# The low half of x by TensorE and ScalarE, the value bias and the token order by TensorE, and no copy of the largest scores, in the projection and the linear q, k, v stages

## The chip, the cores and the metric

One NeuronCore of a Trainium2 chip runs the whole program. The time is the device time of one launch in microseconds, and it is compared as a median of several launches. The engines are TensorE (PE; its weight loads are listed as PEld), VectorE (DVE), ScalarE (ACT), GpSimd (POOL) and SyncE (SP), which here only issues DMAs. TensorE's clock has two levels, 1.2 and 2.4 GHz; "granted clock" is its share of full speed (0.5 or 1).

## The reference

Four sublayers, each `x = x + layernorm(f(layernorm(x)))`, on x of 8 x 1024 x 256 floats (8192 tokens):

```python
x = x + ln(softmax_attention(ln(x)) @ w_proj)        # 16 heads of 16, causal
x = x + ln(moe64(ln(x)))                             # sigmoid scores, 6 of 64 experts, shared expert
x = x + ln(linear_attention(ln(x)) @ W_out + b_out)  # q, k = elu(...) + 1.0001, causal sums
x = x + ln(moe8(ln(x)))                              # softmax scores, 4 of 8 experts, shared expert
```

Two pieces matter here. After the first attention comes its projection, the residual sum, the next layernorm and the choice of six experts:

```python
scores = sigmoid(ln(x) @ router_weight.T)
_, top_idx = top_k(scores + expert_bias, 6)
probs = take(scores, top_idx) / (sum + 1e-20)
```

And the linear attention begins with its q, k and v:

```python
qkv = ln(x) @ W_qkv + b_qkv
q = elu(q * 16 ** -0.5) + 1.0001
k = elu(k) + 1.0001
```

## The kernel before

The program is seven phases, one after the other, with a barrier between them. Two of them are touched: `phase_project_route` (tiles named `prj_`) and `phase_linear_qkv` (tiles named `lqk_`). Both walk over 16 blocks of 512 tokens (8 batches x 2 halves). Each engine has its own instruction list, written by hand as a function `stages(...)`, and `pipeline` runs it so that several blocks are in flight: in one step of `prj` the stages a, b, c, d work on four successive blocks, in one step of `lqk` the stages a, b, c on three. Semaphores alone tie the lists together, and each engine does its list strictly in the written order; the order of the work is therefore exactly the order of the code, for SP's DMA issues too.

Products are made to near full precision from two halves. `xh` is x rounded to fp32r, `xl` is what is left (x - xh), and `product` adds three fp32r matmuls per 128 rows of contraction (high x high, high x low, low x high). The normal x comes out of a layernorm with tokens on the partitions (`xn`), TensorE turns it (8 transposes of 128 x 128, `xn_ready` to `xn_turned`) into `t_ps` in PSUM, ScalarE copies `t_ps` to `xh`, and VectorE then forms `xl = t_ps - xh` (lines 1052 and 1743), signalled by `xl_ready`.

**A step of prj, engine by engine.** TensorE: the projection of block b into `y_ps` (24 matmuls of 256 columns, waits for `al_ready`), the router logits of block d into `l_ps` (24 matmuls of 64 columns, waits for `xl_ready`), the 8 transposes of block c, then `r_ps` for the mask of block d (waits for `choice_ready`). ScalarE: the sigmoid `sc` (waits for the logits), four normalisations `xn`, the high half `ah` of the attention output, four normalisations `yn`, `xh`, and the copy `rt` of `r_ps`. VectorE: statistics of x and of y, two scalings `nmr`, the division `att`, the choice of the experts (`choose`: bias added into `sb`, MAX8, a copy of the K largest values into `pick`, MATCH_REPLACE8, mask), `al = att - ah`, `xl`, and the weights (`weigh`). `pick` holds the six largest scores and two values of 3e38; `sb` has two spare columns that hold 3e38, which the replacing operation uses up in their place.

**A step of lqk.** TensorE: q and k of block c (`qk`: 4 x 6 matmuls of 512 columns, waits for `xl_ready`), the 8 transposes of block b, v of block c (`vp`: 24 matmuls of 256 columns), then 8 transposes of phi(k) of block c (line 1832), which write `t_ps` too and so wait for `xl_ready` of block b, and for `phi_done`. ScalarE: exponentials 0 and 1 of `qk`, four normalisations `xn`, exponentials 2 and 3, four normalisations `yn`, `xh`, and the copy `kt` of the turned phi(k). VectorE: the residual sum `x2` (waits for `yn`), the statistics of x2 and of the summed expert output `a`, two scalings, twice (min of the exponentials, two `phi`), the bias added to v (`vo`, line 1735), and `xl` (line 1743). POOL sums the three parts of `a`. A block's tokens lie as four runs of 128 (`t`, `q`: token 4 q + t stands at column 128 t + q); `phi` has to be stored in token order, and VectorE restores it when it reads `qk` and `ex`:

```python
def in_order(a):
    return a.rearrange("p (t q) -> p q t", t=TPB)
...
e.scalar_tensor_tensor(phi[:, j, k].rearrange("p (q t) -> p q t", t=TPB),
                       in_order(qk[:, k]), bqk1[:, k:k + 1], in_order(ex[:, k]),
                       ALU.add, ALU.max).then_inc(phi_done, 1)
```

SP, in one step of lqk: the store of x2 and the four loads of the next block (after `inputs_used`), the store of v (after `vo_ready`), and the stores of phi(q), phi(k) and kt (after `kt_ready`). Since the list is strict, the loads of a step stand behind the kt stores of the step before.

## Time and profile before

| | us |
|---|---|
| median of three launches | 3262.55 (3261.11 to 3276.6) |
| the profiled launch: its own time | 3258.48 |
| the profiled launch: its span, first to last instruction | 3256.8 |
| PE busy in the span | 2842.0 (87%) |
| DVE busy | 2225.7 (68%) |
| ACT busy | 1603.0 (49%) |
| POOL busy | 731.5 (22%) |

prj takes its 16 blocks between about 1130 and 1344 us of the span, lqk between about 1693 and 1956 us. A period is the time between two successive steps of such a stage: the first `xl` of prj starts at 1135.2 and the sixteenth at 1336.8, and in lqk they start at 1696.6 and 1939.4, so that 15 periods are 201.6 us (13.4 each) and 242.8 us (16.19 each). In the timeline rows further down the columns are: start in us, length in us (from the first start to the last end, where rows are merged with xN), engine, line, operation, output<-inputs with sizes, and in brackets the idle time of that engine just before it and what ended it. A matmul's length contains its latency, so matmuls in a stream overlap: how fast they go is read from the distance of their starts.

### The profile page before, as it was taken

Reading aid. Unit: us, or ns where it says so; the run is one execution under the profiler, and the core shown is the slowest. Engines: PE = TensorE matmul, PEld = TensorE weight load, DVE = VectorE, ACT = ScalarE, POOL = GpSimd, SP = SyncE. Lnnn points to the kernel's source line nnn. Section 1 sums busy time; section 2 is a strip of 40 time slices with the busy share of each in tenths; the row PEclk is TensorE's granted clock in tenths of the full one; section 3 lists DMA queues with packets and bytes.
Section 4 is the critical chain, followed back from the end, with each engine's and each line's share of the span. In section 5 each row is a group of like instructions: output and inputs, shape, how many; then the busy total and the mean of one; then the engine's idle time right before and its main releaser. Section 6 shows DMA issues by size and latency. Waiting matters only on the chain. (4 is left out here: it accounts for less than half of the span.)

```text
span 3256.8 us, 59136 instructions
## 1 busy us (share of the span) xinstructions
PE 2842.0 (87%) x20033; PEld 2062.9 (63%) x20033; DVE 2225.7 (68%) x6134; ACT 1603.0 (49%) x2446; POOL 731.5 (22%) x882
## 2 busy tenths in 40 slices
PE   7959999999999387689947777998399999999998
PEld 6834444444444276578836664555388888888887
DVE  6768999999997388663338883444466666666664
ACT  3506777777777244333325544544244444444443
POOL 1022222222222133247744422222000000000000
PEclk9959999999999666699968888999699999999999
DMA  6984556666662377648857867653432424243331
GB/s 244 330 153 83 108 115 112 112 112 116 112 110 65 127 270 269 214 138 225 221 165 269 296 228 228 183 162 100 132 99 74 122 65 117 78 102 92 90 86 46
DMA packets 342662, 485.87 MB, mean 149 GB/s; under 512 B 58832, under 2 KB 203248, under 8 KB 342384
## 3 DMA queue, kind: packets, MB, share of 16 engines
q1 hardware_dynamic: 331776, 468.94, 52.1%
q0 software_dynamic: 10240, 14.16, 2.3%
q8 instruction: 85, 1.39, 0.2%
q10 hardware_dynamic: 496, 0.84, 0.1%
q14 instruction: 65, 0.53, 0.1%
HBM read 278.77 MB, written 204.53 MB: 148 GB/s over the span
## 5 line engine op out<-in xcount | busy, mean ns | idle before, releaser
L551 ACT ACTIVATE att_pr<-att_e_ps 128x1024 f32<-128x1024 f32 (+2 forms) x640 | 567.3, 938 | 203.8 <-PE att_e_ps L603 203.8
L579 PE MATMUL att_m_ps<-att_ks,att_qs 63*128 63x512 f32 (+3 forms) x1536 | 465.9, 433 | 40.2 <-PEq L41 31.7
L513 DVE CUSTOM_DVE_ANT_0 att_kept<-att_m_ps,att_causal 128x256 f32<-128x256 f32 (+3 forms) x1024 | 448.5, 488 | 50.3 <-DVEq L41 21.9
L579 PEld LDWEIGHTS att_m_ps<-att_ks,att_qs 63*128 63x128 f32 x1536 | 234.3, 189 | 370.6 <-DVE att_mx L516 148.5
L492 POOL TENSOR_SCALAR_AFFINE_SELECT att_pr<-att_pr 128x256 f32<-128x256 f32 (+1 forms) x384 | 181.4, 485 | 698.0 <-PEq L594 694.5
L516 DVE TENSOR_REDUCE att_mx<-att_m_ps 128x1 f32<-128x512 f32 x512 | 323.3, 684 | 21.5 <-PE att_m_ps L579 17.5
L623 PE MATMUL att_o_ps<-att_pr,att_vs 128*32 128x512 f32 (+3 forms) x3072 | 328.7, 501 | 3.7 <-issue 2.0
L2604 ACT ACTIVATE fin_hh<-fin_hid 128x512 fp32r<-128x512 f32 x192 | 121.4, 632 | 399.8 <-DVE fin_hid L2450 302.2
L603 PE MATMUL att_e_ps<-att_qs,att_ks 64*128 64x512 f32 (+3 forms) x1536 | 269.1, 376 | 6.7 <-ACT att_pr L551 3.3
L2343 POOL TENSOR_TENSOR fin_rs<-fin_ve,fin_mhalf 128x4 f32<-128x4 f32 x48 | 48.4, 1007 | 928.6 <-POOLq L41 928.6
L2446 DVE TENSOR_TENSOR fin_hid<-fin_gate,fin_u_ps 128x512 f32<-128x512 f32 x192 | 131.5, 685 | 136.4 <-ACT fin_gate L2598 82.9
L738 PE MATMUL fin_f_ps<-fin_fhd,fin_hh 128*128 128x256 f32 x768 | 219.5, 286 | 0.2 <-DVE fin_hl L2465 0.2
L738 PE MATMUL fin_f_ps<-fin_fhd,fin_hl 128*128 128x256 f32 x768 | 216.3, 282 | 0.0
L738 PE MATMUL fin_f_ps<-fin_fld,fin_hh 128*128 128x256 f32 x768 | 216.2, 282 | 0.0
L2465 DVE TENSOR_TENSOR fin_hl<-fin_hid,fin_hh 128x512 fp32r<-128x512 f32 x192 | 132.5, 690 | 104.5 <-ACT fin_hh L2604 100.8
L1949 DVE TENSOR_TENSOR lin_am<-lin_a_ps,lin_tri 128x512 f32<-128x512 f32 x128 | 88.5, 692 | 143.5 <-PE lin_a_ps L2032 143.5
L603 PEld LDWEIGHTS att_e_ps<-att_qs,att_ks 64*128 64x128 f32 x1536 | 150.1, 187 | 38.8 <-ACT att_pr L551 13.5
L738 PE MATMUL fin_u_ps<-fin_xh,fin_fhu 128*128 128x512 f32 x384 | 153.0, 398 | 0.0
L738 PE MATMUL fin_g_ps<-fin_xh,fin_fhg 128*128 128x512 f32 x384 | 152.5, 397 | 0.0
L738 PE MATMUL fin_g_ps<-fin_xh,fin_flg 128*128 128x512 f32 x384 | 151.9, 396 | 0.0
L738 PE MATMUL fin_u_ps<-fin_xh,fin_flu 128*128 128x512 f32 x384 | 151.6, 395 | 0.0
L738 PE MATMUL fin_u_ps<-fin_xl,fin_fhu 128*128 128x512 f32 x384 | 151.5, 394 | 0.0
(332 smaller groups left out, 6921.2 us busy)
## 6 DMA issues: line engine op xcount, KB each, us to landing
fin_raw<-weights SPq DMA_DIRECT2D x32, 1024.0 KB, 9.6
att_qs<-q_high SPq DMA_DIRECT2D x128, 128.0 KB, 5.2
att_ks<-k_high SPq DMA_DIRECT2D x128, 128.0 KB, 6.5
attended<-att_ot SPq DMA_DIRECT2D x64, 256.0 KB, 8.5
acc<-att_zero SPq DMA_DIRECT2D x64, 256.0 KB, 2.2
moe_w<-w SPq DMA_DIRECT2D x128, 128.0 KB, 3.4
lqk_a<-acc SPq DMA_DIRECT2D x32, 512.0 KB, 6.0
attended<-lin_ot SPq DMA_DIRECT2D x32, 512.0 KB, 3.7
```

Source lines behind the costliest of these rows:

```text
L492: e.affine_select(out=blk, in_=blk, compare_op=ALU.is_ge, fill=0.0, base=0, pattern=lead + [[1, P]], channel_multiplier=-1).then_inc(maske ...
L513: e.tensor_tensor_reduce(kept[:, n % MBUF, 0:w], m_ps[:, n % MBUF, 0:w], causal[:, BLK - w:], 1.0, -3e38, ALU.add, ALU.max, mx[:, h, at, q ...
L516: e.reduce_max(mx[:, h, at, q:q + 1], m_ps[:, n % MBUF, 0:w], AX.X).then_inc(m_free, 1)
L551: e.activation(out, src, ACT.Exp).then_inc(exp_done, 1)
L579: e.matmul(m_ps[:, (2 * i + n) % MBUF, 0:w], qs[rows, j, p, q * P:(q + 1) * P], ks[rows, j, p, h * BLK:h * BLK + w], start=True, stop=True ...
L603: i = e.matmul(e_ps[:, s % 2, n, m * w:(m + 1) * w], ks[rows, j, p, k * P:(k + 1) * P], qs[rows, j, p, (h + 1) * BLK - w:(h + 1) * BLK], s ...
L623: i = e.matmul(o_ps[32 * hd:32 * hd + 32, BLK - w:BLK], vs[:, j, k, hd * VW:hd * VW + 32], pr[:, u % NPR, hd // 2, hd % 2, 0:w], start=k = ...
L738: i = e.matmul(out, a, b, start=first and n == 0, stop=last and n == len(terms) - 1, **kw)
L1949: e.tensor_tensor(am[:, n % 2, 0:F // 2].rearrange("p (r h) q -> p r h q", h=2), a_ps[:, 0:2, 0:2 * P].rearrange("p r (h q) -> p r h q", h=2),
L2446: product_ = e.tensor_tensor(hid[:, c % 2], gate[:, c % 2], u_ps[:, c % 2], ALU.mult)
L2465: e.tensor_tensor(hl[:, c % 3], hid[:, c % 2], hh[:, c % 3].bitcast(fp32), ALU.subtract).then_inc(hl_ready, 1)
L2604: e.activation(hh[:, c % 3], hid[:, c % 2], ACT.Copy).then_inc(hh_ready, 1)
```

## The change

In both stages:

- The turning of `xn` is no longer a transpose instruction but a plain fp32 matmul with the identity as the moving operand, which opens an accumulation group in `t_ps`. When ScalarE has read `xh` out of `t_ps`, TensorE adds `-1 * xh` to `t_ps` (two matmuls of 512 columns, stationary operand `minus`, waiting for `xh_ready`, signal `rest_ready`), and ScalarE copies what is left into `xl`. VectorE's subtraction is gone.
- These two matmuls stand at the end of TensorE's step in prj, and between v and the transposes of phi(k) in lqk. The new ScalarE copy stands last in prj's step; in lqk it stands after `xh` and `vo` and before `kt`.

In prj alone: `pick` and its copy are gone. MAX8 looks at `sb` with its two spare columns of 3e38, so that `top` holds these two and the six largest scores.

In lqk alone: the matmuls of q and k read their moving operand through `in_order`, so that `qk` and `ex` come out in token order and VectorE reads and writes plain rows. The bias of v is added by TensorE (two more matmuls of one contraction row and 256 columns for each of the four `vp` tiles), and `vo` becomes a ScalarE copy from PSUM; the new semaphore `v_read`, which SP raises, keeps TensorE from writing `vp` too early. The bias is loaded as one row, no longer as 128.

```diff
+                e.wait_ge(pe_consts, 1)
+                step(e.tensor_scalar(minus[:], ident[:], -1.0, None, ALU.mult))
                 step(e.memset(sb[:, :, E:E + 8 - K], 3e38))
...
-                        e.max(top[:, t], sb[:, t, 0:E])
+                        e.max(top[:, t], sb[:, t])
                     step.settle()
-                    step(e.tensor_copy(pick[:, :, 0:K], top[:, :, 0:K]))
 
                     for t in range(TPB):
-                        e.match_replace(rep[:, t], pick[:, t], sb[:, t], -3e38)
+                        e.match_replace(rep[:, t], top[:, t], sb[:, t], -3e38)
...
-                    if c is not None:
-                        e.wait_ge(xh_ready, 1)
-                        e.tensor_tensor(xl[:, c[1]], t_ps[:], xh[:, c[1]].bitcast(fp32), ALU.subtract
-                                        ).then_inc(xl_ready, 1)
-                        take(e, (xh_ready, 1))
...
+                    if c is not None:
+                        e.wait_ge(rest_ready, 1)
+                        e.activation(xl[:, c[1]], t_ps[:], ACT.Copy).then_inc(xl_ready, 1)
+                        take(e, (rest_ready, 1))
...
-                            i = e.transpose(t_ps[:, k, t * P:(t + 1) * P], src[:, t, k * P:(k + 1) * P], ident[:])
+                            i = e.matmul(t_ps[:, k, t * P:(t + 1) * P], src[:, t, k * P:(k + 1) * P], ident[:], start=t == 0,
+                                         stop=t == TPB - 1)
...
+                    if c is not None:
+                        e.wait_ge(xh_ready, 1)
+                        for k in range(KC):
+                            i = e.matmul(t_ps[:, k], minus[:], xh[:, c[1], k], start=False, stop=True,
+                                         skip_group_check=True)
+                        i.then_inc(rest_ready, 1)
+                        take(e, (xh_ready, 1))
...
-                                e.scalar_tensor_tensor(phi[:, j, k].rearrange("p (q t) -> p q t", t=TPB),
-                                                       in_order(qk[:, k]), bqk1[:, k:k + 1], in_order(ex[:, k]),
-                                                       ALU.add, ALU.max).then_inc(phi_done, 1)
-                        e.wait_ge(v_ready, 1)
-                        for f in range(2):
-                            cols = slice(f * P, (f + 1) * P)
-                            i = e.tensor_tensor(vo[:, j, f].rearrange("p t (h d) -> p t h d", d=VW)[:, :, :, 0:HD],
-                                                vp[:, :, cols].rearrange("p t (h d) -> p t h d", d=HD),
-                                                bv[:, cols].rearrange("p (h d) -> p h d", d=HD).unsqueeze(1)
-                                                .broadcast_to((P, TPB, NH // 2, HD)), ALU.add)
-                        i.then_inc(vo_ready, 1)
-                        take(e, (exp_ready, 4), (v_ready, 1))
-                    if b is not None:
-                        e.wait_ge(xh_ready, 1)
-                        e.tensor_tensor(xl[:, b[1]], t_ps[:], xh[:, b[1]].bitcast(fp32), ALU.subtract
-                                        ).then_inc(xl_ready, 1)
-                        take(e, (xh_ready, 1))
+                                e.scalar_tensor_tensor(phi[:, j, k], qk[:, k], bqk1[:, k:k + 1], ex[:, k], ALU.add,
+                                                       ALU.max).then_inc(phi_done, 1)
+                        take(e, (exp_ready, 4))
...
                     if c is not None:
+                        e.wait_ge(v_ready, 1)
+                        for f in range(2):
+                            cols = slice(f * P, (f + 1) * P)
+                            i = e.activation(vo[:, c[1], f].rearrange("p t (h d) -> p t h d", d=VW)[:, :, :, 0:HD],
+                                             vp[:, :, cols].rearrange("p t (h d) -> p t h d", d=HD), ACT.Copy)
+                        i.then_inc(vo_ready, 1)
+                    if b is not None:
+                        e.wait_ge(rest_ready, 1)
+                        e.activation(xl[:, b[1]], t_ps[:], ACT.Copy).then_inc(xl_ready, 1)
+                        take(e, (rest_ready, 1))
+                    if c is not None:
                         e.wait_ge(k_turned, 1)
                         e.activation(kt[:, c[1]], t_ps[:].rearrange("p f (t c) -> p f t c", t=TPB), ACT.Copy
                                      ).then_inc(kt_ready, 1)
-                        take(e, (qk_ready, 4), (k_turned, 1))
...
-                                    (lambda k: xh[:, j, k], lambda k: xl[:, j, k]), KC).then_inc(qk_ready, 1)
+                                    (lambda k: in_order(xh[:, j, k]), lambda k: in_order(xl[:, j, k])), KC
+                                    ).then_inc(qk_ready, 1)
                         take(e, (xl_ready, 1))
                     if b is not None:
                         for t in range(TPB):
                             e.wait_ge(xn_ready, t + 1)
                             for k in range(KC):
-                                i = e.transpose(t_ps[:, k, t * P:(t + 1) * P], xn[:, t, k * P:(k + 1) * P], ident[:])
+                                i = e.matmul(t_ps[:, k, t * P:(t + 1) * P], xn[:, t, k * P:(k + 1) * P], ident[:], start=t == 0,
+                                             stop=t == TPB - 1)
                         i.then_inc(xn_turned, 1)
                         take(e, (xn_ready, TPB))
                     if c is not None:
+                        e.wait_ge(v_read, 1)
                         for t in range(TPB):
                             cols = slice(t * P, (t + 1) * P)
-                            i = product(e, vp[:, t], (lambda k: xh[:, j, k, cols], lambda k: xl[:, j, k, cols]),
-                                        (lambda k: wh[:, k, 2 * C:3 * C], lambda k: wl[:, k, 2 * C:3 * C]), KC)
+                            product(e, vp[:, t], (lambda k: xh[:, j, k, cols], lambda k: xl[:, j, k, cols]),
+                                    (lambda k: wh[:, k, 2 * C:3 * C], lambda k: wl[:, k, 2 * C:3 * C]), KC, last=False)
+                            e.matmul(vp[:, t], one[:], bvh[:], start=False, stop=False)
+                            i = e.matmul(vp[:, t], one[:], bvl[:], start=False, stop=True)
                         i.then_inc(v_ready, 1)
+                        take(e, (v_read, 1))
+                    if b is not None:
+                        e.wait_ge(xh_ready, 1)
+                        for k in range(KC):
+                            i = e.matmul(t_ps[:, k], minus[:], xh[:, b[1], k], start=False, stop=True,
+                                         skip_group_check=True)
+                        i.then_inc(rest_ready, 1)
+                        take(e, (xh_ready, 1))
                     if c is not None:
                         if b is not None:
                             e.wait_ge(xl_ready, 1)
```

The first place is TensorE's list in prj, one step inside the loop; `prj_r_ps` is the mask's product, `prj_t_ps` the turned x, `prj_y_ps` the projection of the next step.

```order
 L738 MATMUL prj_l_ps<-prj_wh,prj_xl 128x64
 L1126 MATMUL prj_t_ps<-prj_ident,prj_xn 128x128 x8
-L1155 MATMUL prj_r_ps<-prj_digits,prj_mask 64x32 x4
+L1156 MATMUL prj_r_ps<-prj_digits,prj_mask 64x32 x4
+L1162 MATMUL prj_t_ps<-prj_xh,prj_minus 128x512 x2
 L738 MATMUL prj_y_ps<-prj_wh,prj_ah 128x256
```

The two matmuls on `xh` have moved in ahead of the projection; before, the projection followed the mask's product directly.

The second place is ScalarE's list in lqk, one step inside the loop, before the change (`ex` exponentials, `kt` the copy of the turned phi(k)):

```order
L1759 ACTIVATE lqk_ex<-lqk_qk,lqk_bqk 128x512 x2
L1770 ACTIVATE lqk_xn<-lqk_x,lqk_nmr,lqk_rs 128x256 x4
L1759 ACTIVATE lqk_ex<-lqk_qk,lqk_bqk 128x512 x2
L1781 ACTIVATE lqk_yn<-lqk_a,lqk_nmr,lqk_rs 128x256 x4
L1787 ACTIVATE lqk_xh<-lqk_t_ps 128x1024
L1791 ACTIVATE lqk_kt<-lqk_t_ps 128x1024
```

And the same step of ScalarE's list after the change:

```order
L1766 ACTIVATE lqk_ex<-lqk_qk,lqk_bqk 128x512 x2
L1777 ACTIVATE lqk_xn<-lqk_x,lqk_nmr,lqk_rs 128x256 x4
L1766 ACTIVATE lqk_ex<-lqk_qk,lqk_bqk 128x512 x2
L1788 ACTIVATE lqk_yn<-lqk_a,lqk_nmr,lqk_rs 128x256 x4
L1794 ACTIVATE lqk_xh<-lqk_t_ps 128x1024
L1800 ACTIVATE lqk_vo<-lqk_vp 128x32x16 x2
L1805 ACTIVATE lqk_xl<-lqk_t_ps 128x1024
L1809 ACTIVATE lqk_kt<-lqk_t_ps 128x1024
```

`vo` (two copies) and `xl` (one) now stand between `xh` and `kt`. The third place is TensorE's list in lqk, the end of v and the beginning of the next q and k, before:

```order
L738 MATMUL lqk_vp<-lqk_wh,lqk_xl 128x256
L1832 MATMUL lqk_t_ps<-lqk_ident,lqk_phi 128x128 x8
L738 MATMUL lqk_qk<-lqk_xh,lqk_wh 128x512
L738 MATMUL lqk_qk<-lqk_xl,lqk_wh 128x512
L738 MATMUL lqk_qk<-lqk_xh,lqk_wl 128x512
```

and after (`bvh`, `bvl` the halves of the bias row, `one` a row of ones):

```order
L738 MATMUL lqk_vp<-lqk_wh,lqk_xl 128x256
L1847 MATMUL lqk_vp<-lqk_bvh,lqk_one 128x256
L1848 MATMUL lqk_vp<-lqk_bvl,lqk_one 128x256
L1854 MATMUL lqk_t_ps<-lqk_xh,lqk_minus 128x512 x2
L1864 MATMUL lqk_t_ps<-lqk_ident,lqk_phi 128x128 x8
L738 MATMUL lqk_qk<-lqk_xh,lqk_wh 128x512
```

The bias's matmuls close each `vp` tile, and the two on `xh` come between v and the transposes of phi(k). The q and k rows read alike before and after: the list does not show that their moving operand is now read in another order.

## Rows read from the trace of the kernel before

**Rows 1.** Busy time by stage (prj, then lqk), TensorE clock, DMA share, GB/s
```profile
core 0: us, PE busy (x) PEld busy (x) DVE busy (x) ACT busy (x) POOL busy (x), PEclk, DMA share, GB/s
1140.00:1333.00 193.00, 151.37 (x889) 133.74 (x888) 159.81 (x601) 88.88 (x169) 63.16 (x42) 0.65 0.75 260
1700.00:1940.00 240.00, 185.16 (x948) 155.31 (x947) 211.59 (x440) 131.86 (x211) 101.67 (x55) 0.88 0.74 271
```
**Rows 2.** Timeline of lqk, VectorE, one step
```profile
1796.77 2.31 DVE L1711 TENSOR_TENSOR lqk_x<-lqk_x,lqk_yn 128x1024 f32<-128x1024 f32 x1
...
1804.78 0.16 DVE L756 SCALAR_TENSOR_TENSOR lqk_nmr<-lqk_mv,lqk_rs 128x4 f32<-128x4 f32 x1 [0.98 <-POOL lqk_rs L1686]
...
1808.48 2.12 DVE L1729 SCALAR_TENSOR_TENSOR lqk_phi<-lqk_qk,lqk_bqk,lqk_ex 128x512 f32<-128x512 f32 x2
1810.52 1.28 DVE L1735 TENSOR_TENSOR lqk_vo<-lqk_vp,lqk_bv 128x512 f32<-128x512 f32 x2
1811.72 1.22 DVE L1743 TENSOR_TENSOR lqk_xl<-lqk_t_ps,lqk_xh 128x1024 fp32r<-128x1024 f32 x1
```
**Rows 3.** Timeline of lqk, TensorE, the same step and the next one's start
```profile
1798.22 0.78 PE L738 MATMUL lqk_qk<-lqk_xh,lqk_wh 128*128 128x512 f32 x1
...
1801.14 0.40 PE L738 MATMUL lqk_qk<-lqk_xl,lqk_wh 128*128 128x512 f32 x1
...
1804.88 0.39 PE L738 MATMUL lqk_qk<-lqk_xh,lqk_wl 128*128 128x512 f32 x1
1805.11 1.29 PE L1817 MATMUL lqk_t_ps<-lqk_ident,lqk_xn 128*128 128x128 f32 x8
1806.16 0.36 PE L738 MATMUL lqk_vp<-lqk_wh,lqk_xh 128*128 128x256 f32 x1
...
1812.99 1.24 PE L1832 MATMUL lqk_t_ps<-lqk_ident,lqk_phi 128*128 128x128 f32 x8 [3.76 <-DVE lqk_xl L1743]
1813.98 0.48 PE L738 MATMUL lqk_qk<-lqk_xh,lqk_wh 128*128 128x512 f32 x1
```
**Rows 4.** Groups by line and shape, lqk: VectorE reads in token order
```profile
L1729 DVE SCALAR_TENSOR_TENSOR lqk_phi<-lqk_qk,lqk_bqk,lqk_ex 128x512 f32<-128x512 f32 x64 | 69.4, 1127 | 1.1
```
**Rows 5.** The same view of the first q, k, v stage, PSUM read in order
```profile
L216 DVE TENSOR_TENSOR qkv_ol<-qkv_qk,qkv_oh 128x512 fp32r<-128x512 f32 x64 | 41.4, 684 | 9.5 <-ACT qkv_oh L243 9.5
L243 ACT ACTIVATE qkv_oh<-qkv_qk 128x512 fp32r<-128x512 f32 x64 | 38.2, 598 | 46.3 <-PE qkv_qk L738 44.2 <-DMA values<-qkv_vo 2.1
```
**Rows 6.** Timeline of the expert stage, TensorE, plain fp32 matmuls (two passes each)
```profile
1504.39 1.03 PE L1530 MATMUL moe_eh_ps<-moe_xt,moe_w 128*128 128x96 f32 x8
```
**Rows 7.** Timeline of lqk, ScalarE
```profile
1803.83 2.08 ACT L1770 ACTIVATE lqk_xn<-lqk_x,lqk_nmr,lqk_rs 128x256 f32<-128x256 f32 x4 [0.63 <-DVE lqk_nmr L756]
...
1808.93 1.01 ACT L1787 ACTIVATE lqk_xh<-lqk_t_ps 128x1024 fp32r<-128x1024 f32 x1
```
**Rows 8.** Timeline of lqk: SP's issue of the last part of a
```profile
1805.54 0.46 SPq L1635 DMA_DIRECT2D lqk_a<-shared  x1
```
**Rows 9.** Timeline of lqk, POOL: the sum of a that follows
```profile
1811.70 2.36 POOL L1677 TENSOR_TENSOR lqk_a<-lqk_a 128x1024 f32<-128x1024 f32 x1 [6.95 <-DMA lqk_a<-shared]
1814.13 3.23 POOL L1678 TENSOR_TENSOR lqk_a<-lqk_a 128x1024 f32<-128x1024 f32 x1
```
**Rows 10.** Timeline of prj, TensorE, one step
```profile
1202.17 0.58 PE L738 MATMUL prj_y_ps<-prj_wh,prj_ah 128*128 128x256 f32 x1 [0.41 <-DVE prj_al L1048]
...
1207.25 0.19 PE L738 MATMUL prj_l_ps<-prj_wh,prj_xh 128*128 128x64 f32 x1
...
1211.40 2.17 PE L1126 MATMUL prj_t_ps<-prj_ident,prj_xn 128*128 128x128 f32 x8 [1.39 <-ACT prj_xn L1083]
1214.60 1.06 PE L1155 MATMUL prj_r_ps<-prj_digits,prj_mask 128*64 128x32 f32 x8 [1.03 <-DVE prj_mask L1014]
1216.07 0.58 PE L738 MATMUL prj_y_ps<-prj_wh,prj_ah 128*128 128x256 f32 x1 [0.41 <-DVE prj_al L1048]
```
**Rows 11.** Timeline of prj, ScalarE, the same step
```profile
1215.83 1.02 ACT L1103 ACTIVATE prj_xh<-prj_t_ps 128x1024 fp32r<-128x1024 f32 x1 [0.25 <-issue]
```

More of the change, by code:

```diff
@@ L773, in phase_project_route @@
         ident = ph.sb("ident", [P, P])
+        minus = ph.sb("minus", [P, P], f32r)
         mhalf = ph.sb("mhalf", [P, TPB])
@@ L839, in phase_project_route @@
         xh_ready = ph.sem("xh_ready")
+        rest_ready = ph.sem("rest_ready")
         xl_ready = ph.sem("xl_ready")
@@ L967, in _ @@
                 split_weights(e, step, wf, wh, wl)
+                e.wait_ge(pe_consts, 1)
+                step(e.tensor_scalar(minus[:], ident[:], -1.0, None, ALU.mult))
                 step(e.memset(sb[:, :, E:E + 8 - K], 3e38))
-                step(e.memset(pick[:, :, K:8], 3e38))
                 e.sem_inc(pe_consts, 1)
@@ L1556, in phase_linear_qkv @@
         bqk1 = ph.sb("bqk1", [P, 4])
-        bv = ph.sb("bv", [P, C])
+        bv = ph.sb("bv", [1, C])
+        bvh = ph.sb("bvh", [1, C], f32r)
+        bvl = ph.sb("bvl", [1, C], f32r)
+        onef = ph.sb("onef", [1, P])
+        one = ph.sb("one", [1, P], f32r)
         ident = ph.sb("ident", [P, P])
+        minus = ph.sb("minus", [P, P], f32r)
         mhalf = ph.sb("mhalf", [P, TPB])
@@ L1601, in phase_linear_qkv @@
         xh_ready = ph.sem("xh_ready")
+        rest_ready = ph.sem("rest_ready")
         xl_ready = ph.sem("xl_ready")
@@ L1609, in phase_linear_qkv @@
         vo_ready = ph.sem("vo_ready")
+        v_read = ph.sem("v_read")
         x2_stored = [ph.sem(f"x2_stored{j}") for j in range(2)]
@@ L1701, in _ @@
                 split_weights(e, step, wf, wh, wl)
+                e.wait_ge(pe_consts, 1)
+                step(e.tensor_scalar(minus[:], ident[:], -1.0, None, ALU.mult))
+                split_weights(e, step, bv, bvh, bvl)
+                step(e.memset(onef[:], 1.0))
+                step(e.tensor_copy(one[:], onef[:]))
                 e.sem_inc(pe_consts, 1)
-                e.wait_ge(ones_ready, 1)
                 step.close()
@@ L1752, in _ @@
                 e.wait_ge(bias_ready, 1)
+                e.wait_ge(ones_ready, 1)
                 for j in range(2):
@@ L1792, in stages @@
                                      ).then_inc(kt_ready, 1)
-                        take(e, (qk_ready, 4), (k_turned, 1))
+                        take(e, (qk_ready, 4), (v_ready, 1), (k_turned, 1))
                 pipeline(e, stages, 3)
@@ L1802, in _ @@
                 e.wait_ge(pe_consts, 2)
+                e.sem_inc(v_read, 1)
                 def stages(a, b, c):
```

4 lines of the change are left out of this document (2 added, 2 removed).

## The prediction

> **What bounds the two stages now.** I read the busy times by stage first, then one step of each stage engine by engine, then the groups by shape for the prices. In lqk VectorE is busy 212 of 240 us and in prj 160 of 193 [rows 1]. In lqk its list closes on itself: its one real wait in a step is 0.98 us for POOL's power, and the sum x2 that opens the step follows `xl` of the step before at once [rows 2]. The period is 16.19 us (15 periods are 242.8 us). Everything else waits for it: TensorE stands 3.76 us before the transposes of phi(k), which need `xl` [rows 3]. Close behind VectorE is the supply of a: SP issued its last part at 1805.54, it landed and POOL began at 1811.70, POOL ended at 1817.36 [rows 8, 9], just when VectorE's statistics need it. In prj the ring is VectorE's choice, `al`, the projection and logits on TensorE, and the sigmoid: the projection starts when `al` is there [rows 10]; the period is about 13.4 to 13.9 us (1202.17 to 1216.07 here).
>
> **lqk, what VectorE loses.** `vo` goes (2 instructions, 1.28 us together) and `xl` (1.22 us) [rows 2]. `phi` took 1127 ns for 512 elements with both operands read in token order [rows 4]; with the PSUM operand alone in that order, VectorE took 684 ns and ScalarE 598 [rows 5]. So the dear part was the read from SBUF in steps of 128 elements, and plain rows should cost about 0.69 us: 4 x 0.44 = 1.75 us less. Together some 4.1 us leave VectorE, whose own ring would fall to about 12 us. It is no longer the bound, whatever else happens.
>
> **lqk, what TensorE and ScalarE gain as work.** TensorE's step after the change, from the end of the phi(k) transposes to the next end:
> - q and k: 24 matmuls at a price s each (below).
> - turning xn as plain fp32: two passes for each of the 8, and a pass costs (1.03 - 0.28) / 7 = 0.107 us by the expert stage's 8 passes [rows 6]; 16 x 0.107 = 1.7 us instead of 1.05.
> - v: from 1806.16 to TensorE's last end, 1812.99 - 3.76 = 1809.23, is 3.07 us for 24 matmuls [rows 3], 2.9 to the start of what follows; the 8 bias matmuls at the same 0.12 each add 0.96: 3.9 us.
> - then a chain through ScalarE: v's end to `vo` about 0.2, two copies of 512 elements at 598 ns [rows 5] 1.2, the new `xl` copy as long as `xh`, 1.0 [rows 7]. The two matmuls on `xh` (0.47 us) run beside `vo` and cost nothing.
> - the transposes of phi(k): 1813.98 - 1812.99 = 1.0 us [rows 3].
>
> Without q and k that is 1.7 + 3.9 + 0.2 + 1.2 + 1.0 + 1.0 = 9.0 us, and 0.1 for hand-overs: 9.1.
>
> **The disputed price s.** At full clock a matmul of 512 columns goes every (1804.88 - 1801.14) / 16 = 0.234 us [rows 3]. No row shows TensorE's moving operand read in steps, so I bound s. From below: the steps cost nothing, s = 0.234. From above: the same pattern costs VectorE 1127 ns for 512 elements [rows 4], s about 1.05. Between them lies TensorE's own load of phi(k) as stationary operand, whose elements stand 16 bytes apart: 8 loads of 128 with their transposes in 0.99 us [rows 3], 0.97 ns an element. If the moving port needs as long for each new place, 512 elements take 0.50 us; VectorE's in-order read, too, was a bit under twice its plain one (1127 to 684). I take s = 0.48, twice the plain price, because it is near both rows that show an SBUF read in steps.
>
> The Trainium skill ("SBUF — State Buffer", section "Specifications (TRN2)") says that a read needs at least two hits in each 16-byte line for full bandwidth; here each element of four bytes lies in another line. That rule speaks against this change, and VectorE's 1127 against 684 ns agrees with it; it names no price, and by it alone s lies above 0.234.
>
> **lqk, the sum.** Period = 9.1 + 24 x 0.48 = 20.6 us, against 16.19: +4.4 us. Over 16 blocks +70 us. The slower clock after TensorE's waits matters little then: a 1.2 GHz matmul of 512 columns takes 0.43 us anyway.
>
> **prj.** VectorE loses `xl` and the small copy, and would close its ring about 2 us earlier. But TensorE's list now puts two matmuls that wait for `xh` ahead of the next projection. Queued behind them are the projection, the logits, and so ScalarE's whole next step. The ring becomes: logits end at 1210.01 (1211.40 - 1.39) [rows 10]; ScalarE does sigmoid, xn, ah, yn and xh, ending at 1216.85 [rows 11], so 6.8 us, less 0.25 because the scaling is ready sooner: 6.6; the two matmuls, 0.9 us at 1.2 GHz or 0.5 at 2.4; projection and logits from 1202.17 to 1210.01, 7.8 us, of which the projection took 5.1 (24 x 0.21, the 1.2 GHz level) and the logits 2.8 [rows 10]. At today's clock: 6.6 + 0.9 + 7.8 = 15.3 us. With everything at 2.4 GHz the projection takes 24 x 0.12 = 2.9 and the ring is 6.6 + 0.5 + 5.6 = 12.7. The granted clock over the stage is 0.65 [rows 1]. The slower turning (up to 16 x 0.21 = 3.4 us at 1.2 GHz) is covered by ah and yn, 2.9 us of ScalarE after the last xn. I take the middle, 14.0: over 15 periods of 13.7 on the mean, +4 us.
>
> The Trainium skill ("TensorE: Matmul & The Clock Gate", section "Part 4: PE-mode transpose") says that transpose-mode work does not count as busy for the clock; plain matmuls in its place would then help the clock up. The trace is in keeping with it: prj's projection starts at 1.2 GHz right after transposes and waits. By the rule the ring would tend to 12.7 rather than 15.3.
>
> What is added once (the matrix `minus`, the split bias row) lies beside the first loads; filling and draining the stages an extra hop costs under 2 us. Sum against the profiled launch's own time: 3258.5 + 70 + 4 = 3332.5; the median of the launches is 4 us above it, so **3336**.
>
> **Rivals.**
> 1. *Reads in steps are free for TensorE.* For it: the stationary loads in steps are hardly dearer than the plain transposes beside them (0.99 us for 8, against 1.05 for the plain ones [rows 3]), so at that pace steps were covered. Against it: rows 4. Then the period of lqk is 9.1 + 5.6 = 14.7 us at full clock; with the slow start that q and k have now (1798.22 to 1805.11, 6.9 us for 24 [rows 3]) it is 16.0. The supply of a holds it too: its loads stand behind kt's stores in SP's list, and kt comes later after the sum x2 than now. I take 15.6: -9 us, with prj's +4 about 3258: no change that can be told (under 0.5%, 16 us, is what I call the same).
> 2. *Free reads and the fast clock.* This is the other side, faster. TensorE's waits shrink, plain matmuls stand where transposes stood, and both stages run at 2.4 GHz: lqk 14.7 (-1.5 x 15.5 = -23 us), prj 12.7 (-1.0 x 15 = -15): 3225. It decides as soon as prj's projection runs 0.12 apart instead of 0.21. Against it: in lqk TensorE still stands some 2 us in each step, and in prj longer.
> 3. *Every step costs TensorE what it costs VectorE.* s = 1.05: 24 x 1.05 + 9.1 = 34.3 us, +18 us a period, about +290 us: 3555. For it: it is the very same pattern. Against it: TensorE's other port takes 0.97 ns an element.
> 4. *Only prj's new wait hurts*, reads free: 15.3 us a period and lqk as now: +25 us, 3287.
>
> **Chances.** Twice the price (anything between 0.35 and 0.6 us) 0.46; free and level 0.18; free and faster, rival 2 and its neighbours, 0.20; rival 3 0.10; rival 4 0.06. Faster by over 0.5%: 0.20; within 0.5%: 0.18; slower: 0.62. The likeliest case alone spans 3300 (s = 0.39) to 3362 (s = 0.54). The range for 8 in 10 goes down over the level case into the faster one, 3238, and up to 3362; rival 3 and the far end of rival 2 stay outside.
>
> **What the changed profile would show.** In lqk: the distance of the q and k matmuls where TensorE runs at full clock (0.48 by the forecast, 0.234 by rivals 1, 2 and 4, about 1 by rival 3); VectorE's `phi` near 0.69 us and VectorE waiting for the exponentials; the period of `xl` 20.6, 14.7 to 16, or 34 us. In prj: the two matmuls on `xh` right after `xh` ends, with the projection following; the distance of its matmuls tells the clock; the period 14.0 with 12.7 and 15.3 as ends. The forecast is wrong if s is at its old price: then nothing in the sum is left that makes the kernel clearly slower, and the sign hangs on TensorE's clock.

## The result, and the profile after

The kernel after takes **3298.7 us** (median of four launches, 3294.0 to 3303.0), the kernel before beside it 3262.1: a ratio of 1.0115, 95% interval 1.0092 to 1.0138. It is slower, as forecast, but by 37 us and not by 74; 3298.7 lies inside the range. The profiled launch has a span of 3293.0 us, 36.2 more than before. By first and last instruction of each stage that is prj +12.1 us (268.7 to 280.8), lqk +14.5 (292.6 to 307.2), and +9.3 in the linear attention stage (304.9 to 314.2), whose code is the same; the others are level within 2 us. Two launches of the experiments below were disturbed, one of e5 (12036 us) and the profiled one of e8 (5005 us): the ratios leave them out, and e8's steps are read from its repetition e10.

Busy time of the kernel after in prj, lqk and linear attention, with the columns of [rows 1], then linear attention in the kernel before:
```profile
1140.00:1345.00 205.00, 164.33 (x1045) 155.26 (x1044) 166.03 (x579) 103.21 (x185) 61.89 (x43) 0.76 0.73 251
1700.00:1960.00 260.00, 235.07 (x1216) 180.10 (x1217) 146.23 (x406) 167.86 (x264) 97.39 (x59) 0.97 0.71 258
1988.00:2302.00 314.00, 287.15 (x3808) 172.99 (x3808) 127.13 (x258) 148.11 (x256) 82.18 (x133) 0.90 0.52 162
```
```profile
1962.00:2267.00 305.00, 279.55 (x3808) 169.59 (x3808) 127.06 (x258) 148.38 (x256) 82.37 (x133) 0.92 0.54 167
```
In lqk VectorE has fallen from 212 of 240 us [rows 1] to 146 of 260, and TensorE has risen from 185 of 240 to 235 of 260, at a clock of 0.97 instead of 0.88. The bound has moved as forecast.

One step of lqk on TensorE, which answers to [rows 3]:
```profile
1813.82 0.52 PE L738 MATMUL lqk_qk<-lqk_xh,lqk_wh 128*128 128x512 f32 x1
1814.18 0.44 PE L738 MATMUL lqk_qk<-lqk_xl,lqk_wh 128*128 128x512 f32 x1
...
1820.38 0.45 PE L738 MATMUL lqk_qk<-lqk_xh,lqk_wl 128*128 128x512 f32 x1
1820.67 1.95 PE L1837 MATMUL lqk_t_ps<-lqk_ident,lqk_xn 128*128 128x128 f32 x16
1822.37 0.36 PE L738 MATMUL lqk_vp<-lqk_wh,lqk_xh 128*128 128x256 f32 x1
...
1827.04 0.28 PE L738 MATMUL lqk_vp<-lqk_wh,lqk_xl 128*128 128x256 f32 x1
1827.25 0.38 PE L1847 MATMUL lqk_vp<-lqk_bvh,lqk_one 1*128 1x256 f32 x1
1827.48 0.27 PE L1848 MATMUL lqk_vp<-lqk_bvl,lqk_one 1*128 1x256 f32 x1
1827.68 0.73 PE L1854 MATMUL lqk_t_ps<-lqk_xh,lqk_minus 128*128 128x512 f32 x2
1829.84 1.23 PE L1864 MATMUL lqk_t_ps<-lqk_ident,lqk_phi 128*128 128x128 f32 x8 [1.43 <-ACT lqk_xl L1805]
1830.83 0.52 PE L738 MATMUL lqk_qk<-lqk_xh,lqk_wh 128*128 128x512 f32 x1
```
From one step's q to the next's it is 17.01 us, and 14 of the 15 distances between `xl` copies are 17.0 (mean 17.07). The q and k matmuls go every (1820.38 - 1814.18) / 22 = 0.282 us: the reads in token order cost 0.05 us each over the 0.234 of [rows 3]. The two one-row matmuls at a tile's end stand 0.21 and 0.23 us behind their forerunners, and the next is 0.20 behind, where v's own stand 0.12 apart.

What ScalarE does at that step's end, and the groups of `phi` and of the sum x2 (columns: line, engine, operation, names, count | busy us, mean ns | idle before):
```profile
1827.79 1.09 ACT L1800 ACTIVATE lqk_vo<-lqk_vp 128x512 f32<-128x512 f32 x2 [3.36 <-PE lqk_vp L1848]
1828.76 1.03 ACT L1805 ACTIVATE lqk_xl<-lqk_t_ps 128x1024 fp32r<-128x1024 f32 x1
```
```profile
L1749 DVE SCALAR_TENSOR_TENSOR lqk_phi<-lqk_qk,lqk_bqk,lqk_ex 128x512 f32<-128x512 f32 x60 | 42.3, 746 | 1.1
L1731 DVE TENSOR_TENSOR lqk_x<-lqk_x,lqk_yn 128x1024 f32<-128x1024 f32 x14 | 17.0, 1215 | 0.0
```
`phi` is at 746 ns instead of 1127 [rows 4], near the 690 that the forecast used. The sum x2 takes 1.22 us in nearly every step, where the step of [rows 2] had 2.31.

One step of prj on TensorE and ScalarE, which answers to [rows 10, 11]:
```profile
1207.51 1.22 PE L1162 MATMUL prj_t_ps<-prj_xh,prj_minus 128*128 128x512 f32 x2 [2.28 <-ACT prj_xh L1099]
1208.53 0.42 PE L738 MATMUL prj_y_ps<-prj_wh,prj_ah 128*128 128x256 f32 x1
...
1213.65 0.22 PE L738 MATMUL prj_l_ps<-prj_wh,prj_xh 128*128 128x64 f32 x1
...
1222.90 0.73 PE L1162 MATMUL prj_t_ps<-prj_xh,prj_minus 128*128 128x512 f32 x2 [1.40 <-ACT prj_xh L1099]
1223.47 0.28 PE L738 MATMUL prj_y_ps<-prj_wh,prj_ah 128*128 128x256 f32 x1
1223.59 0.28 PE L738 MATMUL prj_y_ps<-prj_wl,prj_ah 128*128 128x256 f32 x1
```
```profile
1206.43 1.02 ACT L1099 ACTIVATE prj_xh<-prj_t_ps 128x1024 fp32r<-128x1024 f32 x1 [0.25 <-issue]
1221.83 1.02 ACT L1099 ACTIVATE prj_xh<-prj_t_ps 128x1024 fp32r<-128x1024 f32 x1 [0.25 <-issue]
```
The wait for `xh` stands where it was expected, 1.3 to 2.3 us in nearly every step, and the projection follows at either level: 5.1 us for 24 matmuls (0.21 apart) in this step, 0.12 apart in the next. Distances of the steps are 12.7 to 14.9 us, mean 14.23, against 13.44 before.

### The profile page after: what moved, and what is told of

Its sections match the earlier page's. It is cut to its first block and busy times, and to the rows that moved or that the text cites. A ratio compares the mean times of both kernels' runs of the same rounds, so it can differ in the third digit from the quotient of the medians.

```text
span 3293.0 us, 60087 instructions
## 1 busy us (share of the span) xinstructions
PE 2915.9 (89%) x20481; PEld 2112.9 (64%) x20481; DVE 2157.3 (66%) x6059; ACT 1651.5 (50%) x2510; POOL 719.4 (22%) x882
## 3 DMA queue, kind: packets, MB, share of 16 engines
q0 software_dynamic: 10240, 14.16, 2.4%
## 5 line engine op out<-in xcount | busy, mean ns | idle before, releaser
L516 DVE TENSOR_REDUCE att_mx<-att_m_ps 128x1 f32<-128x512 f32 x512 | 323.4, 684 | 21.5 <-PE att_m_ps L579 17.4
```

Of the source, the lines that this page charges most:

```text
L516: e.reduce_max(mx[:, h, at, q:q + 1], m_ps[:, n % MBUF, 0:w], AX.X).then_inc(m_free, 1)
```

## The experiments

All ratios are to the kernel before, run beside it on the same chip, with 95% intervals. Stage lengths and steps are of one profiled launch of each.

| run | what | ratio | prj step | lqk step | linear attention, us |
|---|---|---|---|---|---|
| before | | 1 | 13.44 | 16.19 | 304.9 |
| after | | 1.0115 (1.0092 to 1.0138) | 14.23 | 17.07 | 314.2 |
| e1 | after, VectorE restores the order | 1.0124 (1.0105 to 1.0143) | 14.23 | 16.93 | 315.3 |
| e2 | after, no value bias | 1.0006 (0.9989 to 1.0023) | 14.32 | 15.11 | 311.1 |
| e3 | after, prj of before | 1.0081 (1.0060 to 1.0102) | 13.44 | 17.50 | 306.2 |
| e4 | before, order by TensorE, no pick copy | 0.9961 (0.9948 to 0.9975) | 13.35 | 15.53 | 308.8 |
| e5 | after, bias matmuls of 128 rows | 1.0065 (1.0044 to 1.0086) | 14.18 | 15.65 | 320.3 |
| e6 | before, turning by plain matmuls | 1.0017 (0.9997 to 1.0036) | 13.56 | 16.27 | 306.2 |
| e7 | after, low half early | 1.0043 (1.0023 to 1.0064) | 14.16 | 15.41 | 320.9 |
| e8 | put together | 1.0010 (0.9991 to 1.0029) | | | |
| e9 | e4 with prj of after, low half early | 0.9960 (0.9941 to 0.9978) | 13.35 | 15.28 | 304.8 |
| e10 | e8 again | 1.0009 (0.9989 to 1.0029) | 13.44 | 15.29 | 320.0 |
| e11 | after again | 1.0141 (1.0115 to 1.0167) | 14.30 | 17.07 | 330.9 |
| e12 | after, TensorE kept busy at linear attention's start | 1.0126 (1.0101 to 1.0150) | 14.40 | 17.40 | 315.4 |

### e1: what do the reads in token order cost?

```diff
-    (lambda k: in_order(xh[:, j, k]), lambda k: in_order(xl[:, j, k])), KC
+    (lambda k: xh[:, j, k], lambda k: xl[:, j, k]), KC
-    e.scalar_tensor_tensor(phi[:, j, k], qk[:, k], bqk1[:, k:k + 1], ex[:, k], ALU.add, ALU.max)
+    e.scalar_tensor_tensor(phi[:, j, k].rearrange("p (q t) -> p q t", t=TPB), in_order(qk[:, k]),
+                           bqk1[:, k:k + 1], in_order(ex[:, k]), ALU.add, ALU.max)
```


> The kernel after, with one part undone: in the linear q, k, v stage TensorE reads xh and xl as they lie, and VectorE's phi restores the token order again. Theory A (TensorE sets the linear stage's step of 17.0 us in the kernel after): its 24 passes per step go from 0.283 back to 0.234 us, 1.2 us less per step, so about -19 us (near 3280), although VectorE's phi goes from 746 back to 1127 ns. Rival B (the step is set by a ring through VectorE and ScalarE): phi's four extra 0.38 us lie on it, and the kernel gets up to 24 us slower (near 3322). Rival C: neither is on the path, same time within 5 us.

Measured: the same time (3 us more by the ratios, which is noise), and steps of 17.1 us once the stage has settled. That is rival C's number, but not for its reason. TensorE in e1:
```profile
1820.56 1.98 PE L1864 MATMUL lqk_t_ps<-lqk_ident,lqk_phi 128*128 128x128 f32 x8 [1.43 <-ACT lqk_xl L1806]
1822.19 0.77 PE L738 MATMUL lqk_qk<-lqk_xh,lqk_wh 128*128 128x512 f32 x1
1822.77 0.63 PE L738 MATMUL lqk_qk<-lqk_xl,lqk_wh 128*128 128x512 f32 x1
1823.19 0.52 PE L738 MATMUL lqk_qk<-lqk_xh,lqk_wl 128*128 128x512 f32 x1
1823.55 0.39 PE L738 MATMUL lqk_qk<-lqk_xh,lqk_wh 128*128 128x512 f32 x1
1823.78 0.39 PE L738 MATMUL lqk_qk<-lqk_xl,lqk_wh 128*128 128x512 f32 x1
```
```profile
1720.00:1900.00 180.00, 165.70 (x877) 137.21 (x876) 133.07 (x286) 118.11 (x189) 68.38 (x42) 0.91 0.77 280
```
The matmuls are back at 0.23 us, so 24 x 0.05 = 1.2 us are gained in each step. But after the same idle time of 1.43 us the clock is at its 1.2 GHz level: the transposes of phi take 1822.19 - 1820.56 = 1.63 us instead of 0.99, and the first three matmuls stand 0.36 to 0.58 apart instead of 0.27 to 0.36. In this stretch the kernel after holds 1.00, e1 0.91: e1 has a stretch of 3.4 us at 1.2 GHz in every step, the kernel after has none. TensorE works less and slower, and the two cancel: in this kernel the reads in order cost nothing net. Why the clock falls in the one and not in the other, after the same wait, no run shows.

### e2 and e5: what does the value bias cost?

e2 leaves the value bias out of the result:
```diff
-    e.matmul(vp[:, t], one[:], bvh[:], start=False, stop=False)
-    i = e.matmul(vp[:, t], one[:], bvl[:], start=False, stop=True)
```


> The kernel after without the eight one-row matmuls per step that add the value bias (the bias of v is left out of the result). Theory A: by the trace they cost about 2.5 us of TensorE's 17.0 us step, not the 0.96 us of the prediction, so up to 2.5 x 16 = 40 us go, less where ScalarE or VectorE is late next (15.5 us or so a step): 3260 to 3275. Rival B: they cost by their columns, 8 x 0.12 us x 16 = 15 us: near 3284. Rival C: TensorE is not what sets the step: within 5 us of the kernel after.

The step falls from 17.07 to 15.11 us, the time by 0.0109 of the kernel before, 36 us. Theory A holds (it had 15.5 us for the step): without the eight matmuls the rest of the change makes lqk shorter than it was (276.4 us against 292.6), and they alone make it longer.

e5 keeps them and fills their rows:
```diff
-    bvh = ph.sb("bvh", [1, C], f32r)       # also bv, bvl, and one and onef as [1, P]
+    bvh = ph.sb("bvh", [P, C], f32r)       # also bv, bvl, and one and onef as [P, P]
-    step(e.memset(onef[:], 1.0))
+    step(e.memset(onef[:], 1.0 / P))
```


> The kernel after with the value bias added by the same eight matmuls per step, but with all 128 rows filled: each row of the stationary operand holds 1/128 and each row of the moving operand the whole bias. Columns and count stay. Theory A (what costs is that a one-row matmul stands between 128-row ones: a tile of v takes 1.335 us instead of 0.71 + 2 x 0.118): the step falls by 8 x 0.19 = 1.5 us, about 25 us in all, near 1.004 of the kernel before. Rival B (any second pair of operands at the end of an accumulation costs that much): no change, near 1.012. Rival C: the one-row matmuls are cheap and their omission gained through ScalarE's copies: no change either, and the timeline would still show 0.71 + 0.63.

Measured: steps of 15.6 us, 1.4 less than the kernel after for 128 times the multiplications; lqk lost 21 us, the ratio 0.0050 or 16 us, as linear attention took 320 us. Theory A, by the step. The end of a tile of v in e5:
```profile
1800.36 0.28 PE L738 MATMUL lqk_vp<-lqk_wh,lqk_xl 128*128 128x256 f32 x1
1800.47 0.28 PE L1847 MATMUL lqk_vp<-lqk_bvh,lqk_one 128*128 128x256 f32 x1
1800.59 0.27 PE L1848 MATMUL lqk_vp<-lqk_bvl,lqk_one 128*128 128x256 f32 x1
1800.70 0.28 PE L738 MATMUL lqk_vp<-lqk_wh,lqk_xh 128*128 128x256 f32 x1
```
All stand 0.12 us apart. So it was the one row: with it, the pair and the change back cost 0.63 us a tile instead of 0.24. That is shown for these shapes; which step of the engine makes it so is not.

### e3 and e4: the parts by themselves

e3 has the linear stage of the kernel after and the projection stage of the kernel before.

> The linear q, k, v stage of the kernel after, the projection stage of the kernel before. Theory A (each stage's price is its own): the projection stage falls from 281 to 269 us, 12 us less than the kernel after: near 3287, and the linear attention stage stays at 314 us. Rival B: the 9 us in the unchanged linear attention stage come from the projection stage's shift in time (the clock's low stretches fall elsewhere): they go as well, near 3278. Rival C: the later stages give the 12 us back.

0.0034 less than the kernel after, 11 us, which is hardly more than the uncertainty of such a difference (about 0.003). The time is theory A's, but its stages are not: prj falls by 13.5 us (280.8 to 267.3), linear attention by 8 (to 306.2, rival B's number), and lqk, whose code is that of the kernel after, takes 313.8 us instead of 307.2, with a mean step of 17.50 us. So prj's share, 12 to 14 us by its stage lengths, rests on those lengths; the ratio alone does not measure it. Linear attention is taken up below.

e4 is the kernel before with `phi` and the q and k matmuls of the kernel after (the lines of e1, the other way round) and `top` in place of `pick`.

> The kernel before with two of the change's parts alone: no copy of the largest scores, and the token order by TensorE's reads (VectorE's phi plain); the xl subtractions and the value bias stay with VectorE. Theory A (the step of 16.2 us before is set by VectorE's ring, which loses 4 x 0.38 us, while TensorE's 24 passes get 0.05 us longer each, 1.2 us): the ring holds the wait for the first two q passes only, so 1.0 to 1.5 us less per step, 16 to 24 us in all, near 3243. Rival B: the longer passes lie on the ring too, and what is left is 0.3 us per step: 3257. Rival C: TensorE's reads cost more than phi gives back: over 3266.

0.9961, 13 us faster than before: the token order by TensorE's reads pays where VectorE is the bound. The lqk step fell by 0.66 us, between theory A and rival B, for TensorE still waits for VectorE's `xl` ahead of `phi`'s transposes, 2.51 us where it was 3.76 [rows 3] (39.4 us over 15 steps, where it was 53.9):
```profile
1817.64 1.23 PE L1829 MATMUL lqk_t_ps<-lqk_ident,lqk_phi 128*128 128x128 f32 x8 [2.51 <-DVE lqk_xl L1739]
```
Dropping the copy of the largest scores is worth 0.09 us in a settled step of prj: the distances alternate between 13.53 and 13.81 us, where they were 13.63 and 13.90. (In e10, with the same prj, they are 13.55 and 13.81, but its first steps are longer and its mean is again 13.44.)

### e6: do plain matmuls help the clock?

```diff
-    i = e.transpose(t_ps[:, k, t * P:(t + 1) * P], src[:, t, k * P:(k + 1) * P], ident[:])
+    i = e.matmul(t_ps[:, k, t * P:(t + 1) * P], src[:, t, k * P:(k + 1) * P], ident[:],
+                 start=t == 0, stop=t == TPB - 1)        # both stages
```


> The kernel before with one part alone: both stages turn xn by plain matmuls with the identity instead of transposes; everything else as before, xl by VectorE. Theory A: in the linear stage TensorE has 2.5 us of idle time a step, so 0.4 us more in the turning costs nothing there; in the projection stage, where two thirds of the time is at 1.2 GHz, the turning is 3.5 us long at that clock and lies on the ring, no more than 0.3 us a step: ratio 1.000 to 1.002. Rival B (plain matmuls count as activity where transposes do not, and raise the clock of the stage): the projection stage's granted clock rises from 0.62 and its step falls by up to 0.7 us: ratio 0.996 to 0.998. Rival C: the turning is a main part of what the projection stage lost (0.8 us a step): ratio 1.004.

Busy times and clock of e6 in prj, over the stretch of [rows 1]:
```profile
1140.00:1333.00 193.00, 147.72 (x992) 141.87 (x990) 158.15 (x595) 87.75 (x167) 62.27 (x41) 0.72 0.75 257
```
The granted clock rose from 0.65 to 0.72, as rival B says, but the step did not fall: 13.56 us, and the ratio, 1.0017, is theory A's. The Trainium skill ("TensorE: Matmul & The Clock Gate", section "Part 4: PE-mode transpose") says that transposes do not count as busy; by that rule the clock should rise, and the trace agrees. But the plain matmuls also are twice as many (16 passes for 8 transposes), and this run does not separate their kind from their number. What the higher clock does not give here is time; that the stage's ring closes elsewhere is my reading of it.

### e7 and e9: the low half formed earlier

e7, in lqk: TensorE does the two matmuls on `xh` ahead of v's last tile, and ScalarE copies `xl` ahead of `vo`. (`rest` waits for `xh_ready`, adds `-1 * xh` to `t_ps` and raises `rest_ready`.)
```diff
     for t in range(TPB):
+        if b is not None and t == 3:
+            rest()
         cols = slice(t * P, (t + 1) * P)
```


> The kernel after with only the order changed in the linear stage: TensorE forms the low half of x ahead of the last of the four tiles of v, and ScalarE copies it out ahead of the values, not behind them. Theory A (TensorE's chain sets the step, and its 1.43 us of idle time waiting for ScalarE's xl copy is part of it): the idle time goes, 1.4 x 16 = 23 us less, ratio near 1.005. Rival B (the wait for ScalarE's values copy takes its place, or the clock falls instead): a third of that or nothing, 1.009 to 1.012.

Step 15.41 us, 1.7 less. TensorE in e7 has no idle time left, at full clock:
```profile
1720.00:1900.00 180.00, 179.91 (x966) 140.40 (x965) 128.62 (x310) 131.07 (x203) 75.80 (x45) 1.00 0.81 295
```
Theory A holds for the stage: lqk takes 282.5 us, 24.7 less than after and 10 less than before. TensorE's own list is the step: the idle time taken out of it (1.43 us a step) comes off. The ratio fell by 0.0072, 23 us. That it did not fall below 1 is prj's 10 us (278.8 against 268.7) and linear attention's 16 (below).

e9, in prj, with the linear stage of e4: the two matmuls stand between the second and third tile of the next block's projection, and ScalarE's copy at the start of its turn.
```diff
     for t in range(TPB):
+        if d is not None and t == 2:
+            rest()
```


> The projection stage of the kernel after with one thing moved: TensorE forms the low half of x in the middle of the next block's y (after two of its four tiles), and ScalarE copies it out at the start of its turn; the linear stage is that of the kernel before with token order by TensorE's reads (its ratio was 0.9961). Theory A (what the projection stage lost is TensorE's wait of 1.3 to 2.3 us for ScalarE's xh): the wait goes, VectorE keeps the subtraction that it lost, and the stage's step falls below the 13.4 us of the kernel before, to 12 to 13 us: ratio 0.988 to 0.993. Rival B (VectorE's and ScalarE's ring sets the step whatever TensorE waits for): 13.4 us as before, ratio 0.996. Rival C (the later y_ready costs more than the wait did): 14.2 us or more, ratio 1.000.

prj's step is 13.35 us, as in e4: rival B. The wait for `xh` was what prj lost (14.2 goes back to 13.35), but VectorE's missing subtraction wins nothing beyond that. TensorE now waits for ScalarE's `ah`, yn and xn instead (waits of e9 from 1140 to 1330 us: total, times, longest):
```profile
PE prj_t_ps L1125 <- ACT prj_xn L1082: 15.6, 15, 2.1
PE prj_y_ps L738 <- ACTq L1097: 9.3, 7, 1.4
```

### e8 and e10: put together

prj of before without the copy; lqk with TensorE's reads in order, the low half early, and the bias by VectorE as before.

> A version put together from the parts that pay. Projection stage of the kernel before without the copy of the largest scores. Linear stage: token order by TensorE's reads, low half of x by TensorE ahead of v's last tile and ScalarE's copy, value bias by VectorE as before. Theory A: TensorE's step is 6.85 (q, k) + 1.8 (turning) + 2.9 (v) + 0.6 + 1.0 = 13.2 us, VectorE has 10.3 us of work, ScalarE 10; the step comes to 13.5 to 14.5 us, 16 x 1.7 to 2.7 less than the kernel before: ratio 0.987 to 0.992. Rival B: the loads and GpSimd's sums bind (with the bias left out the step was 14.7 to 15.9 us and the transfers' share 0.80): step about 15, ratio 0.994. Rival C: VectorE's order (values, then the next x2) makes xn late, step 15.5 or more: 0.996 or above.

> The same version as in the run before of this name (projection stage of the kernel before without the copy; linear stage with TensorE's reads in token order, low half of x ahead of v's last tile, bias by VectorE), since its profiled execution was disturbed and shows no step. Theory A: the step of the linear stage is 13.5 to 14.5 us, and the linear attention stage after it gives back what it gained. Rival B: the step itself is 15 us or more, and VectorE's values ahead of x2 or the loads set it.

The ratio is 1.001 both times, outside theory A's range. The step of lqk is 15.3 us, rivals B and C: VectorE's values stand ahead of x2, which runs beside GpSimd's sum in this step and takes 2.56 us instead of 1.2, and TensorE waits for xn (0.80 us here) and `xh` (1.19) behind it. That this order is what holds the step is read from the trace; no run changed it. e10, VectorE and GpSimd:
```profile
1800.19 1.29 DVE L1737 TENSOR_TENSOR lqk_vo<-lqk_vp,lqk_bv 128x512 f32<-128x512 f32 x2 [2.24 <-PE lqk_vp L738]
1801.40 2.56 DVE L1714 TENSOR_TENSOR lqk_x<-lqk_x,lqk_yn 128x1024 f32<-128x1024 f32 x1
```
```profile
1800.51 2.36 POOL L1678 TENSOR_TENSOR lqk_a<-lqk_a 128x1024 f32<-128x1024 f32 x1 [7.03 <-DMA lqk_a<-shared]
```
The 13.6 us that lqk still gained (279.0 us) went again in linear attention, 320.0 us instead of 304.9, as theory A of e10 had it.

### e11 and e12: the stage that nobody changed

> The kernel after once more, for a second trace. Theory A (the 9 us in the unchanged linear attention stage belong to the change, through the clock): the stage takes 312 to 317 us again. Rival B (they are the variation of one execution): 305 to 309 us, while the projection and linear stages stay at 280 and 307.

> The kernel after with 64 idle matmuls (the mask with itself, into a buffer that is overwritten) that TensorE does at the start of the linear attention stage while the first loads arrive; the stage is otherwise untouched. In both traces of the kernel after its first low stretch of the clock lasts from before the stage's first matmul to 20 to 41 us into it. Theory A (the stage's length follows from how long the clock stays at 1.2 GHz after TensorE's pauses): the first low stretch is short, half its time in the stage is gained, 6 to 15 us, so the stage takes 300 to 308 us and the ratio to the kernel before falls from 1.0115 and 1.0141 to 1.007 to 1.010. Rival B (a debt: what is held at 2.4 GHz here is given back in the stage's later low stretches): these grow, the stage stays at 314 or more and the ratio at 1.0115 or more. Rival C: the idle matmuls delay the first real ones and the stage gets longer by their overlap, 1 to 3 us.

Linear attention in e11 and in e3:
```profile
1987.00:2318.00 331.00, 303.14 (x3808) 180.58 (x3808) 127.14 (x258) 148.72 (x256) 82.19 (x133) 0.84 0.49 154
```
```profile
1978.00:2284.00 306.00, 281.28 (x3808) 170.40 (x3808) 127.05 (x258) 148.50 (x256) 82.24 (x133) 0.92 0.54 166
```
Neither expectation of e11 holds: the stage takes 330.9 us, more than both ranges, so two launches of the same kernel differ by 17 us here, while prj (282.5) and lqk (307.5) come out as before.

These are the same 3808 matmuls; only the clock differs. TensorE is busy nearly throughout and pauses three times, at the start and about 80 and 160 us in; after each pause the clock stays at 1.2 GHz for 3 to 48 us. Over thirteen traces the stage's length from its first matmul on, less half the time at 1.2 GHz, is 274 to 280 us (276 both in the kernel before and after), while the length itself goes from 293 to 319. The ratios, which rest on several launches each, follow these stage lengths, so the loss is not the noise of one launch alone: e7 and e10 gained 10 and 14 us in lqk against the kernel before and lost 16 and 15 here.

e12 did shorten the first low stretch, 27 us in the kernel after and 48 in e11, to 10. The later low stretches did not grow (24 and 14 us, against 14 and 31 in the kernel after and twice 31 in e11), so nothing of rival B's debt is seen, though its numbers for the stage and the ratio came true. But the 64 matmuls ended 6.4 us after ScalarE had the first operands ready, and that ate the gain (the stage is 297.6 us long from its first real matmul, 315.4 in all). The ratio, 1.0126, says nothing of the stage, as lqk took 315.0 us in this launch, 8 more than in the kernel after. It is rival C beside A, and decides little. What makes the low stretches long in one kernel and short in another stays open. Of the runs whose lqk held the clock at 2.4 GHz all but some 35 to 55 us (after, e2, e5, e7, e10, e11) all six had 311 to 331 us here; those with more time at 1.2 GHz had 305 to 309 (before, e3, e4, e6, e9), but e1 and e12 315 with 84 and 65 us. That speaks for something given back later and does not show it.

## Why the prediction was right, and where its sizes were off

The direction was right and the time lies in the range, but with much luck. Of the 74 us forecast, 70 were to come from lqk, by the reads; lqk gave 14.5, prj 12, and linear attention, which was not in the sum, 9.

- **The bound moves from VectorE to TensorE in lqk.** Right, with all of VectorE's savings near their forecast sizes. e7 shows that TensorE's list is then the step.
- **The price s.** Taken 0.48, measured 0.282: the term was 24 x 0.48 = 11.5 us and came to 6.85, so 4.7 us a step, 75 us in all, too much. It lies below the likeliest case (0.35 to 0.6), near the old price, 0.234, which the forecast had named as its sign of being wrong. Between the ends 0.234 and 1.05 I took the row that I held for the nearest, the loads of phi(k). It was a bad neighbour: the plain transposes of xn, whose loads have no steps, are no faster (1.05 us for 8, against 0.99 [rows 3]), so its 0.97 ns an element was not the price of the steps, which was my own argument in rival 1. The rule of the Trainium skill ("SBUF — State Buffer", section "Specifications (TRN2)") that two hits in each 16-byte line are needed for full bandwidth holds here in sign only: four times the lines cost VectorE 1127 against 746 ns (there the PSUM operand was in token order too), and TensorE 0.282 against 0.234 us.
- **v and its bias.** Taken 3.9 us, measured 1827.68 - 1822.37 = 5.3. I gave the eight matmuls v's pace; they cost 2.5 us, not 0.96 (e5: 1.4 us of it for having one row). This error of 1.4 us a step, 23 us in all, ran against the first, so that the total came closer than its terms. That is luck.
- **The rest of the step**: turning 1.7 us forecast and 1.70 measured, the chain through `vo` and `xl` 2.4 and 2.16, the phi transposes 1.0 and 0.99. Right.
- **prj.** The ring of 12.7 to 15.3 us with 14.0 between: steps of 12.7 to 14.9, mean 14.23, and the wait for `xh` shown as its cause by e9. The sum was too small by my own subtraction: I took 0.3 us over "13.7 on the mean", where the mean before was 13.44. It should have been +8 us; it was +12.
- **The clock.** The forecast held slower starts in lqk for unimportant. In the kernel after they are gone (0.97), and in e1 they are back and cost about 1.2 us a step, as much as the disputed reads.
- **Not in the sum:** linear attention's +9 us, behind the changed stage and through the clock alone.

So the sign rests on another leg than the forecast gave it. With s at its measured price and all else as forecast, the period of lqk is 9.1 + 24 x 0.282 = 15.9 us, 5 us less in all, and prj's +4 makes the kernel level. By the sum it was the reads; by e2 and e3 it is the one-row matmuls (36 us) and the wait for `xh` in prj (11 us), and without these two the change would have been about level with the kernel before (1.0115 - 0.0109 - 0.0034 = 0.997, with 0.003 of uncertainty in each term; the two together were not run). Rival 1's price of the reads was the closest: its step of lqk, 14.7 to 16.0 us, and the 1.4 us of the dearer bias make 16.1 to 17.4.

Of all versions e4 and e9 alone beat the kernel before, by 0.4%. e4 is the simpler one: token order by TensorE's reads, no copy of the largest scores, all else as before.

## What to carry to other kernels

Price every added instruction by a row of its own shape: an addition of one row "for nothing" at the end of an accumulation cost 2.6 times its columns, and the same sum with all rows filled was cheaper. Where a bound between far ends decides the forecast, ask of the neighbour row what paced it before taking its number. Where an engine's list is the step, first look for idle time that another order takes out of it (e7: 1.7 us a step for two matmuls and a copy moved), and count in the stages behind it: in e7 and e10 the next stage lost what was gained, by a clock whose cause stays open.

## What the runs showed of the hardware that I had not expected

- The moving operand read in token order, in steps of 128 elements: 0.282 us for 512 columns against 0.234, far from a quarter of the pace.
- One-row matmuls of 256 columns among 128-row ones: about 0.32 us each with the change back, against 0.12.
- Less work on TensorE can leave the step as it is, through the clock (e1: 1.63 us for transposes that took 0.99).
- In prj of the kernel after an operation on four numbers a partition takes 1.9 us beside GpSimd's sum, where it took 0.17 in e4 (first VectorE, then GpSimd):
```profile
1222.20 1.93 DVE L1026 TENSOR_SCALAR prj_ssum<-prj_ssum 128x4 f32<-128x4 f32 x1
```
```profile
1221.75 2.36 POOL L955 TENSOR_TENSOR prj_xo<-prj_x,prj_yn 128x1024 f32<-128x1024 f32 x1 [4.58 <-ACT prj_yn L1091]
```
It ends with that sum, 1224.1 us. Whether it cost the stage anything no run shows.
